# A 32 by 32 VectorE transpose for the low-rank factor B, and float32r idle products, in a fused two-layer mixing and feed-forward kernel

## What is computed

```python
# x: (32, 64, 1024) float32; itok: (32,) condition numbers 0..15
def cond(x, itok, W):                    # W: (16, 64, 64)
    return einsum('bct,bcd->bdt', x, W[itok])
def ffn0(x, w, b):                       # w: (1024, 1024)
    scale = mean(abs(w), axis=0)
    t = where(abs(w) < 0.05, 0, sign(w)) * scale
    return x @ t + b
def ffn1(x, q, qs, bias, A, B):          # A: (8, 1024), B: (1024, 8)
    w = NF4_LEVELS[q] * qs               # one scale for 64 inputs
    return x @ w.T + bias + 4.0 * (x @ A.T) @ B.T
x = x + ffn0(cond(x, itok, mix0), w0, b0)
x = x + ffn1(cond(x, itok, mix1), ...)
```

## Time and profile before

| | |
|---|---|
| Median of 3 runs | 357.35 us (357.08 to 357.49) |
| The profiled execution | 358.29 us, of which the span is 356.5 us |
| Granted TensorE clock, mean | 0.999 |
| PE busy | 348.7 us, 98% of the span |
| DVE busy | 232.8 us, 65% |
| POOL busy | 233.2 us, 65% |
| ACT busy | 165.5 us, 46% |

### The profile page before, as it was taken

How to read it: one execution, slowest core, us unless ns; L and a number is a source line. 1 busy time by engine, 2 the same in 40 slices (tenths; PEclk the granted TensorE clock), 3 DMA queues, 4 the chain that set the end, 5 groups by cost and what they waited for, 6 DMA issues and landing times.

```text
span 356.5 us, 5523 instructions
## 1 busy us (share of the span) xinstructions
PE 348.7 (98%) x1820; PEld 295.6 (83%) x1820; DVE 232.8 (65%) x354; ACT 165.5 (46%) x298; POOL 233.2 (65%) x153
## 2 busy tenths in 40 slices
PE   6899999999999999999999999999999999999996
PEld 6668788888888888888888888888888888888884
DVE  5689968999999999995859336155362552624523
ACT  2688367878887887772535305013040130411300
POOL 0388999998877987778511666567365673666632
PEclk9999999999999999999999999999999999999999
DMA  6894411753454345324421301505115042150202
GB/s 242 270 340 142 155 31 30 270 205 126 138 165 156 118 153 187 146 71 173 142 103 63 120 0 65 180 0 187 58 64 182 0 162 83 62 181 2 118 29 90
DMA packets 27838, 44.63 MB, mean 125 GB/s; under 512 B 8834, under 2 KB 17026, under 8 KB 27810
## 3 DMA queue, kind: packets, MB, share of 16 engines
q1 hardware_dynamic: 26242, 43.67, 35.3%
q10 hardware_dynamic: 1568, 0.61, 0.6%
HBM read 27.49 MB, written 16.78 MB: 124 GB/s over the span
## 4 chain that ended last, share of the span: by engine, by line
PE 92%; POOL 2%; SPq 1%; DMA 1%; ACT 1%; DVE 1%; issue 1%; POOLq 0%; ACTq 0%
PE acc L1208 37%; PE acc L1170 31%; PE xT L1134 11%; PE acc L1150 6%; PE spare L1134 4%; POOL col_scale L617 2%; PE acc L1236 2%; DMA w_in<-in_L_ffn_w 1%; PE acc L1238 1%; PE xT L1217 1%; SPq L447 0%; SPq L445 0%; SPq L466 0%; ACT w_in L718 0%; PE xT L1225 0%
## 5 line engine op out<-in xcount | busy, mean ns | idle before, releaser
L1170 PE MATMUL acc<-T,hh 128*128 128x512 f32 x192 | 76.0, 396 | 0.0
L1170 PE MATMUL acc<-T,hl 128*128 128x512 f32 x192 | 75.1, 391 | 0.0
L590 POOL TENSOR_TENSOR X<-X,bias 128x1024 f32<-128x1024 f32 x28 | 67.2, 2401 | 11.3 <-PE xT L1134 9.7
L1208 PE MATMUL acc<-W,hh 128*128 128x512 f32 x224 | 71.3, 389 | 0.0
L744 ACT ACTIVATE spare<-q_raw 128x512 f32<-128x512 int32 x96 | 56.0, 599 | 18.6 <-DVE side_p L944 6.3
L1032 DVE TENSOR_TENSOR X<-X,acc 128x512 f32<-128x512 f32 x42 | 28.8, 687 | 40.5 <-PE acc L1208 21.4
L649 POOL TENSOR_TENSOR X<-X,ys 128x512 f32<-128x512 f32 x21 | 26.4, 1286 | 36.6 <-DVE ys L1021 36.6
L1208 PEld LDWEIGHTS acc<-W,hh 128*128 128x128 f32 x224 | 42.1, 188 | 8.7
L1208 PE MATMUL acc<-W,hl 128*128 128x512 f32 x112 | 43.6, 389 | 0.0
L1170 PEld LDWEIGHTS acc<-T,hl 128*128 128x128 f32 x192 | 36.1, 188 | 7.4
L1134 PEld LDWEIGHTS xT<-mix,X 128*128 128x128 f32 x336 | 40.8, 192 | 1.4
(11 more groups left out here) (99 smaller groups left out, 652.1 us busy)
## 6 DMA issues: line engine op xcount, KB each, us to landing
out<-X SPq DMA_DIRECT2D x26, 512.0 KB, 2.9
X<-out SPq DMA_DIRECT2D x16, 512.0 KB, 3.5
X<-in_x SPq DMA_DIRECT2D x12, 512.0 KB, 3.4
q_raw<-in_L_ffn_q_weight SPq DMA_DIRECT2D x16, 256.0 KB, 2.9
w_in<-in_L_ffn_w SPq DMA_DIRECT2D x14, 256.0 KB, 6.6
x_first<-in_x SPq DMA_DIRECT2D x4, 512.0 KB, 4.2
out<-x_first SPq DMA_DIRECT2D x4, 512.0 KB, 4.7
out<-X SPq DMA_DIRECT2D x4, 256.0 KB, 2.0
```

What stands on the lines that cost most here:

```text
L590: pool.tensor_tensor(x_of(g), x_of(g), bias[:, :], ALU.add).then_inc(s_xb, 1)
L1170: mm = pe.matmul(acc[:, bank_of(q), :], a[:, k, :], b, start=(k == 0 and j == 0), stop=(k == KB - 1 and j == len(terms) - 1))
L1208: mm = pe.matmul(acc[:, bank, :], a[:, k, :], w1(part, c, k), start=(k == 0 and j == 0), stop=(k == HB - 1 and j == len(terms) - 1))
```

## The change

B is no longer loaded as 128 partitions of 8 rows with 8 numbers each. It is loaded four times into the four quarters of 32 partitions of an idle buffer (`b_in`, in `ys`), 256 contiguous numbers a partition. VectorE scales it (128x256), casts it into columns 0 to 7 of each 32-wide block of `b_wide`, subtracts to make the low part in quarters 1 and 3, and transposes `b_wide` (128x1024) in squares of 32 by 32 into the first piece of `w_in`, once the sums have read that piece. ScalarE copies the result to `loraB` in one instruction that also reorders the columns. The eight TensorE transposes are gone. Ahead of the first mixing VectorE copies `ident` twice to `loraA` in float32r, before it clears `mix`; TensorE's idle products read `loraA` and are now ten pairs of 128 and 256 columns.

```diff
-    lora_b_v = lora_b.rearrange("(o p) r -> p o r", p=P)
+    Q = 32
+    lora_b_v = lora_b.rearrange("(p o) r -> p (o r)", p=Q)
...
+        b_in = ys[:, F - 1, 0:T // Q * R]
+        b_turned = w_in[:, 0, :]
...
-            act.dma_start(b_raw[:, :, :], lora_b_v).then_inc(s_bin, 16)
+            for r in range(4):
+                act.dma_start(b_in[Q * r:Q * r + Q, :], lora_b_v).then_inc(s_bin, 16)
...
-                    for h in range(NH):
-                        act.wait_ge(s_bT, h + 1)
-                        act.activation(loraB[:, h * BANK:(h + 1) * BANK], flat(h), ACT.Copy
-                                       ).then_inc(s_loraB, 1)
+                    act.wait_ge(s_bT, 1)
+                    act.activation(loraB[:, :].rearrange("p (i o) -> p o i", o=T // Q),
+                                   b_turned.rearrange("p (o i) -> p o i", i=Q), ACT.Copy
+                                   ).then_inc(s_loraB, 1)
...
+            dve.wait_ge(s_ident, 1)
+            for i in range(2):
+                dve.tensor_copy(loraA[:, i * P:(i + 1) * P], ident[:, :]).then_inc(s_identr, 1)
...
-            dve.wait_ge(s_bin, 16)
+            dve.wait_ge(s_bin, 64)
             dve.wait_ge(s_fill, 2)
-            dve.tensor_scalar(b_raw[:, :, :], b_raw[:, :, :], LORA_SCALING, None, ALU.mult
-                              ).then_inc(s_b4, 1)
+            dve.tensor_scalar(b_in, b_in, LORA_SCALING, None, ALU.mult).then_inc(s_b4, 1)
             dve.wait_ge(s_b4, 1)
-            for c in (0, 64):
-                dve.tensor_copy(b_wide[:, :, c:c + R].bitcast(F32R), b_raw[:, :, :]).then_inc(s_b4, 1)
-            dve.wait_ge(s_b4, 3)
-            for c in (32, 96):
-                dve.tensor_tensor(b_wide[:, :, c:c + R], b_raw[:, :, :], b_wide[:, :, 0:R],
+            b4 = b_in.rearrange("p (o r) -> p o r", r=R)
+            dve.tensor_copy(b_wide[:, :, 0:R].bitcast(F32R), b4).then_inc(s_b4, 1)
+            dve.wait_ge(s_b4, 2)
+            for r in (1, 3):
+                rows = slice(Q * r, Q * r + Q)
+                dve.tensor_tensor(b_wide[rows, :, 0:R], b4[rows, :, :], b_wide[rows, :, 0:R],
                                   ALU.subtract).then_inc(s_b4, 1)
+            dve.wait_ge(s_b4, 4)
+            dve.wait_ge(s_sum, KB)
+            dve.transpose(b_turned, b_wide[:, :, :].rearrange("p o c -> p (o c)")).then_inc(s_bT, 1)
...
                 elif g == F:
-                    pe.wait_ge(s_loraB, NH)
+                    pe.wait_ge(s_colscale, NH)
...
-            pe.wait_ge(s_ident, 1)
+            pe.wait_ge(s_identr, 2)
             for _ in range(WARM):
-                pe.matmul(acc[:, 0, 0:P], ident[:, :], ident[:, :], start=True, stop=True)
+                pe.matmul(acc[:, 0, 0:P], loraA[:, 0:P], loraA[:, 0:P], start=True, stop=True)
+                pe.matmul(acc[:, 0, 0:2 * P], loraA[:, 0:P], loraA[:, 0:2 * P], start=True, stop=True)
...
             first(2, 1, 0)
-            turn_b()
             first(2, 1, 1)
...
             pe.wait_ge(s_al, 1)
+            pe.wait_ge(s_loraB, 1)
```

More of the change, by code:

```diff
@@ L233, in build @@
         tok = sb("tok", [1, B], I32)
-        b_raw = sb("b_raw", [P, KB, R], F32)
+        tok_pad = sb("tok_pad", [P, KB * R], F32)
         X = sb("X", [P, XS, T], F32)
@@ L269, in build @@
             a_in = sb("a_in", [P, T], F32, first_use)
-            b_wide = sb("b_wide", [P, KB, P], F32, first_use)
+            b_wide = sb("b_wide", [P, T // Q, Q], F32, first_use)
         with ExitStack() as second_use:
@@ L358, in build @@
         s_ident = sem("s_ident")
+        s_identr = sem("s_identr")
         s_fill = sem("s_fill")
@@ L1218, in column_sums @@
                           start=True, stop=True).then_inc(s_colsum, 1)
-            def turn_b():
-                pe.wait_ge(s_ident, 1)
[L1222 to L1227, removed]
             def turn_w(d):
```

## The result

The changed kernel takes 363.38 us (median of 6 runs, 362.36 to 364.00) against 357.42 before (6 runs, 357.08 to 357.73): 1.0164 times as long, 95% interval 1.0145 to 1.0182. That is slower by 6.0 us. 360.6 was forecast, and the range ended at 361.8. The profiled execution took 364.00 us with a span of 362.2, where before it was 358.29 and 356.5 (5.7 more). Both profiled executions lie above the median of their kernel, by 0.6 and 0.9 us.

A forecast was written before the change was run, and what follows sets the result against it. TensorE, busy 98% of the span, was taken to bound the kernel. Terms of -0.87 (transposes), +0.3 (start) and +3.9 (stall) summed to +3.3, giving 360.6 us on the median, range 356.8 to 361.8.

The forecast's parts named there:

- What bounds the kernel, and that `leave_y(2)` has 0.1 to spare: TensorE bounds, busy 98% of the span; VectorE's `leave_y(2)` ends at 41.06, just before `first(2, 1, 0)` at 41.18.
- The transposes: Removing the eight `turn_b` transposes from TensorE's chain at about 43 us gains 0.87.
- The start: Two casts ahead of clearing `mix` delay SyncE and ScalarE by 0.3 (0.2 to 0.45), all passed on: +0.3.
- The idle products hide behind the mixing's load: Before the first mixing: ten pairs take 4 to 4.8, end at 5.9 to 6.7; 0.4 of lateness hidden, nothing booked.
- Four loads, 0.85 late: ScalarE's four issues from 21.52 make its next sign 0.85 late (0.7 to 1.0), passed on to VectorE and GpSimd.
- VectorE's preparation step by step: At 33 to 44 us, VectorE's instructions wait for gaps between GpSimd's; `leave_y(2)` is 3.1 late, 45.05 with the 0.85.
- A stall of 3.9: TensorE waits 3.9 at `first(2, 1, 0)` for `leave_y(2)`, which ends at 45.05 and is wanted by about 41.1.
- The sum, -0.87 + 0.3 + 3.9 = +3.3, and with it the range up to 361.8: Whole kernel: transposes, start and stall add +3.3, giving 360.6 on the median; range from 356.8 to 361.8.
- a rival on the idle products of the start: Idle products end as late as 9.6 or leave the mixings on the lower clock: about +2; chance 0.05.
- Later: VectorE's lateness is hidden by its 2.74 of idle time: After the stall, VectorE's 2.74 us of idle time before the `leave_y` at 53.92 hides its lateness.
- The copy to `loraB` stands for two of like total: ScalarE's one copy replaces two of like total, with some 10 us of cover; without cover it would cost 1.1.
- The waiting transpose: Rival: VectorE's transpose waits behind `add_bias` to 43.6, stall near 6.5: +5.9, 363.2; chance 0.08.

The follow-up runs named there:

- e11: Kernel before, with three more small loads of B issued by ScalarE into a buffer nobody reads: 359.16 us, 1.005.
- e3: Kernel before, with only the start and idle products changed (two casts ahead of clearing `mix`, float32r pairs): 357.69 us, 1.0004.
- e5: Changed kernel, with the four loads of B issued by SyncE instead of ScalarE: 361.12 us, 1.0117 against the kernel before.
- e6: Changed kernel, with GpSimd waiting for VectorE's `loraA` instruction before its first `add_bias`: 361.85 us, 1.0128 against the kernel before.
- e7: Changed kernel without VectorE's transpose, `loraB` filled from data that is not B's: 362.96 us, 1.0162 against the kernel before.
- e2: Changed kernel, with sixteen extra idle products on TensorE between `first(1, 1, 1)` and `first(2, 1, 0)`: 361.78 us, 1.0125 against the kernel before.
- e1: Changed kernel, with `leave_y(2)` moved ahead of VectorE's preparation of B: 363.12 us, 1.015 against the kernel before.
- e9: Changed kernel, B's loads on SyncE, `leave_y(2)` before B's preparation, `loraA`'s low part behind `leave_y(6)`, `mix` cleared before the casts: 358.01 us, 1.0022 against the kernel before.
- e12: As e9, but with the start and idle products of the kernel before: 357.93 us, 1.0019 against the kernel before.
- e4: Changed kernel with the start and idle products of the kernel before, so only B changed: 362.81 us, 1.014 against the kernel before.
- e8: Changed kernel, B's loads on SyncE, its preparation and `loraA`'s low part behind `leave_y(6)`, ScalarE's copy later, `mix` cleared before the casts: 364.62 us, 1.0205.

## Why the prediction was wrong, and where it was right

- *What bounds the kernel, and that `leave_y(2)` has 0.1 to spare*: right. e11 made it 1.1 late by itself and TensorE waited 1.13.
- *The transposes*, -0.87: their removal is 0.79 by the starts of the products around them. Right.
- *The start*, +0.3: right in SyncE's queue, where `w0` is issued 0.36 later. That all of it is passed on is not shown: e3 can't tell its time from 0.
- *The idle products hide behind the mixing's load*: right in the time, since e3 costs nothing that can be measured. In the change they end within 0.2 of the mixing's start and the mixing is at full pace; in e3 it took 2.52. The profiles show a granted clock of 1.00 all through the idle products, so only the spacing of the passes speaks for a lower one there.
- *Four loads, 0.85 late*: mis-sized. It was 1.1 (1.38 less the 0.28 that was there before), since the last three issues took 0.47 each on ScalarE's queue. The mechanism stands (e5, e11).
- *VectorE's preparation step by step*: right in every step. Cast behind the last sum, the pair split over two gaps, transpose 1.25 (1.15 said) without a turn, `loraA` behind the second `add_bias`. `leave_y(2)` was said to end at 45.05, plus the shift of the start; it ended at 45.06. That the two agree to 0.01 is luck: the issues cost 0.25 more, the shift came on top, and the cast ended 0.5 later than forecast. But GpSimd's second `add_bias`, for whose end `loraA` waits, began before the second subtraction was done, and ended at 43.25, just as forecast. e6 (pair 0.87 instead of 3.93) and e7 (no transpose, no gain) show the turns.
- *A stall of 3.9*: 3.5 as the trace counts idle time, 3.7 between starts. Right.
- *The sum, -0.87 + 0.3 + 3.9 = +3.3, and with it the range up to 361.8*: this is the step that failed. It priced a stall of 3.9 at 3.9. It lacked a term for the clock after the stall: 2.5 in the trace of the changed kernel (1.5 in that of e7), and absent in e2, which has the same lateness and no idleness. With the 2.5 the sum is 5.8; measured were 6.0, and 5.7 between the two traces. I had the clock in a rival on the idle products of the start only, and never asked what TensorE's own new idle time would do. The Trainium skill, page "TensorE: Matmul & The Clock Gate", section "HAM oscillation — how this bites in real kernels", warns of idle gaps that throttle the clock again. This case's trace agrees (0.50 after the 3.5 us of wait), and e5 goes further: its 2.42 is shorter than the gaps that the page warns of, and the clock fell too, so the measurement decides. The case for the term was in the forecast stall itself.
- *Later: VectorE's lateness is hidden by its 2.74 of idle time*: right in result, wrong in reason. That idle time comes after `low_x(4)`, which has a cover of 1.2 at `mixed(5)`. It was hidden because TensorE had been stalled as long. e1 took that stall away and paid the same 3.9 at `mixed(5)`.
- *The copy to `loraB` stands for two of like total*: wrong. It took 2.05 where the two took 1.09, and VectorE waited for ScalarE's next line 1.14 in place of 0.48. Hidden in the changed kernel; in e9 the next waits are about there, but how much of them is this copy's was not tried.
- *The waiting transpose*, a rival with 363.2, comes within 0.2 of the measured number, and is false all the same: the transpose waited for no turn.

What stays open: why e9 and e12 are 0.7 to 0.8 above the kernel before when their added waits (1.0 and 1.1) less 0.8 for the transposes leave some 0.3; the 0.4 of e11 that no row shows; and what decides whether the clock stays low for 3.4 or for 6.8 us after a wait.

## What to carry to other kernels

When a forecast has TensorE idle where it was busy, price the clock as well as the wait: here waits up to 1.7 us cost no clock, those from 2.42 us on did, and 3.5 us of wait cost 6.2 in the trace of the change. When an engine's list becomes longer, the question is not whether the next waiting instruction can be moved ahead of it but what the later ones have to spare; in a kernel where three engines keep pace with TensorE, work taken off TensorE (0.8 here) has to be free on the engine that gets it. And the cost of a small VectorE instruction beside GpSimd's long ones is the turn it misses, so count gaps, not elements.

## What the runs showed of the hardware that I had not expected

- The granted clock fell to 0.50 in or just behind waits of 2.42 us (e5), 3.46 (e7), 3.50 (the change), 3.93 (e1), 4.30 (e4) and 6.2 (e8), and not in waits of 1.13 (e11), 1.0, 1.3 and 1.7 (e6). In e5 it fell only at 44 us, when the products had been running again for 1.1, and in e7 0.3 behind the end of the wait.
- It stayed low for 3.4 us in e5 and e7 and for 6.8 in the change, e1, e4 and e8. TensorE had work without a break for the last 5.5 of the 6.8 in the change. The changed kernel's timed runs fall into two groups at least 0.8 us apart: mean clocks of 0.994, as in the traces of e5 and e7 (0.994 and 0.995), and of 0.989 to 0.991, as in that of the change (0.989).
- ScalarE's copy of 128x1024 that writes with a step of 32 numbers took 2.05; the contiguous copy of the same size (`loraA`) 1.04.
- Two subtractions on 32 partitions (256 numbers each) took a turn with GpSimd each, 3.93 for the pair; without GpSimd beside them, in e6, the pair took 0.87.
